# Weighting the experts' outputs on GpSimd and summing them with one reduction per chunk on VectorE

## The reference

```python
xc = depthwise_conv(x, dw_kernel) + dw_bias                   # 3 taps along the sequence
x1 = x + silu(xc @ pw_w.T + pw_b)
logits = x1 @ router_w.T + router_b                           # 8 experts
top_v, top_i = top_k(logits, 2); top_w = softmax(top_v)
rw = sum(one_hot(top_i, 8) * top_w[..., None], axis=-2)       # 8 weights per token, 6 of them zero
ye = silu(einsum('bsd,eod->bseo', x1, expert_w) + expert_b)   # all 8 experts, dense
combined = einsum('bse,bseo->bso', rw, ye)                    # <- the part that is changed
h = rmsnorm(x1 + combined @ out_w.T + out_b) * norm_w
y = h + gelu(h @ ff_down_w.T + ff_down_b) @ ff_up_w.T + ff_up_b
x = layernorm(x + y)
```

## Time and profile before

| | us |
|---|---|
| three runs, median (lowest to highest) | 3467.42 (3454.39 to 3469.43) |
| profiled execution | 3465.11 |
| its span, first to last instruction | 3463.2 |
| last instruction of `combine`, chunk 0, ends | 2450.20 |
| last instruction of `combine`, chunk 15, ends | 2715.57 |

### The profile page before, as it was taken

One profiled execution on the slowest core, in us unless ns is written; L12 is line 12 of the kernel. 1 busy time (PEld: TensorE's weight loads), 2 busy tenths in 40 slices (PEclk: granted clock), 3 DMA queues, 4 the chain that ended last, 5 costly groups with the idle time before them and its releaser, 6 DMA issues. The chain is left out here.

```text
span 3463.2 us, 83326 instructions
## 1 busy us (share of the span) xinstructions
PE 2800.7 (81%) x28622; PEld 1991.1 (57%) x28638; DVE 2189.8 (63%) x5986; ACT 1821.4 (53%) x3448; POOL 1835.0 (53%) x1742
## 2 busy tenths in 40 slices
PE   2999858988888799826459997996988669996993
PEld 2999746745555466514336664664445436664893
DVE  3122466568887588751458886777899767886124
ACT  0555446445555566502136665775566767662551
POOL 5742764357776555444655545664033755554626
PEclk9999989989998899955579998998899989997997
DMA  9888612001100221117411112221000011222884
GB/s 334 264 261 243 194 50 12 3 27 41 39 36 37 70 78 64 61 51 187 128 41 51 61 46 95 81 88 58 1 1 1 3 29 57 77 67 82 249 255 121
DMA packets 325161, 315.42 MB, mean 91 GB/s; under 512 B 111350, under 2 KB 244889, under 8 KB 324508
## 3 DMA queue, kind: packets, MB, share of 16 engines
q1 hardware_dynamic: 283244, 261.98, 24.6%
q0 software_dynamic: 16384, 33.59, 3.3%
q10 hardware_dynamic: 25264, 16.40, 1.6%
HBM read 167.28 MB, written 60.69 MB: 66 GB/s over the span
## 5 line engine op out<-in xcount | busy, mean ns | idle before, releaser
L938 DVE TENSOR_TENSOR moe_first_tile_y<-moe_first_out_ps,moe_first_expert_w 128x256 f32<-128x256 f32 x85 | 36.0, 424 | 245.5 <-PE moe_first_out_ps L1074 245.5
L1871 POOL TENSOR_TENSOR causal_k_blocks<-causal_k_T,headmask 128x1024 f32<-128x1024 f32 x64 | 121.4, 1899 | 99.6 <-PE causal_scores L1481 94.0
L1871 POOL TENSOR_TENSOR alibi_k_blocks<-alibi_k_T,headmask 128x1024 f32<-128x1024 f32 x64 | 121.3, 1897 | 94.8 <-PE alibi_scores L1481 91.0
L796 POOL DMA_INDIRECT moe_first_token_y<-slot_y,moe_first_slots x128 | 125.2, 978 | 82.4 <-DMA slot_y<-moe_first_tile_y 44.1
L1074 PEld LDWEIGHTS moe_first_out_ps<-moe_first_expert_w,moe_first_hid 128*128 128x128 f32 x1360 | 164.9, 192 | 4.3
L1871 POOL TENSOR_TENSOR full_k_blocks<-full_k_T,headmask 128x1024 f32<-128x1024 f32 x64 | 120.8, 1898 | 85.0 <-PE full_scores L1481 80.0
L1074 PE MATMUL moe_first_out_ps<-moe_first_expert_w,moe_first_hid 128*128 128x128 f32 x1360 | 165.2, 275 | 0.0
L1147 POOL DMA_INDIRECT slot_x<-x_tok,moe_first_slots x128 | 123.9, 968 | 67.3 <-issue 38.1
L3164 PE MATMUL L_ffn_experts<-weights_odd,x_T 128*128 128x512 f32 x256 | 143.1, 643 | 12.4 <-ACT L_ffn_expert_out L3264 11.3
L1871 POOL TENSOR_TENSOR keys_k_blocks<-keys_k_T,headmask 128x1024 f32<-128x1024 f32 x64 | 120.9, 1900 | 46.0 <-PE keys_scores L1481 42.4
L3087 DVE SCALAR_TENSOR_TENSOR L_ffn_combined<-L_ffn_expert_out,L_ffn_mix,L_ffn_combined 128x128 f32<-128x128 f32 x448 | 138.9, 372 | 4.0
(11 more groups left out here) (580 smaller groups left out, 9079.8 us busy)
## 6 DMA issues: line engine op xcount, KB each, us to landing
moe_first_expert_w<-in_L_attn_experts SPq DMA_DIRECT2D x85, 578.0 KB
moe_last_expert_w<-in_L_ffn_experts SPq DMA_DIRECT2D x53, 578.0 KB
moe_first_tile_x<-slot_x SPq DMA_DIRECT2D x85, 128.0 KB, 4.7
slot_y<-moe_first_tile_y SPq DMA_DIRECT2D x85, 128.0 KB
slot_x<-blank ACTq DMA_DIRECT2D x2, 4992.0 KB, 40.4
L_ffn_tile_x<-slot_x SPq DMA_DIRECT2D x32, 256.0 KB, 3.4
slot_y<-L_ffn_tile_y SPq DMA_DIRECT2D x32, 256.0 KB
moe_last_tile_x<-slot_x SPq DMA_DIRECT2D x53, 128.0 KB, 4.0
```

What stands on the lines that cost most here:

```text
L796: pool.indirect_dma_start(y_in[:, p, k, r, :], None, slot_y[part][0:NTS[part] * SLOT_TILE, :], bass.IndirectOffsetOnAxis(slots[:, part, r, ...
L938: dve.tensor_tensor(y_out[:, q, :, :], out_bank[j % 2][:, 0:SLOT_TILE].rearrange("p (s d) -> p s d", s=SPAN), over(wall[:, j % RING, 2 * F ...
L1871: pool.tensor_tensor(k_blocks[:, t.p, :, :], keys.to_broadcast([128, 8, TILE]), lanes.to_broadcast([128, 8, TILE]), ALU.mult).then_inc(spr ...
```

## The change

The multiplication leaves VectorE: GpSimd multiplies `expert_out` in place, one 128x1024 operation per tile (`weigh`), four per chunk. VectorE's `combine` becomes one tensor_reduce over the experts, 128x512 from 128x4096, that reads with the expert axis innermost. `mean_square` moves ahead of `combine` in VectorE's list, and `rms` ahead of the first `weigh` in GpSimd's. `comb_done` counts one per chunk instead of eight.

```diff
@@ vector
+                if c >= 2:
+                    dve.wait_ge(weighed, PER * (c - 1))
                 dve.tensor_scalar(mix[:, c % 2, :, :], twice[:, :, :], 0.5, None, ALU.mult).then_inc(mix_done, 1)
             def combine(c):
                 p = c % 2
-                dve.wait_ge(mix_done, c + 1)
-                dve.wait_ge(expert_done, 2 * PER * (c + 1))
                 if c >= 2:
                     dve.wait_ge(combT_ready, c - 1)
-                for e in range(E):
-                    if e:
-                        dve.wait_ge(comb_done, E * c + e)
-                    for k in range(PER):
-                        w = mix[:, p, k, e:e + 1]
-                        if e == 0:
-                            last = dve.tensor_scalar(combined[:, p, k, :], expert_out[:, p, k, e, :], w, None, ALU.mult)
-                        else:
-                            last = dve.scalar_tensor_tensor(combined[:, p, k, :], expert_out[:, p, k, e, :], w,
-                                                            combined[:, p, k, :], ALU.mult, ALU.add)
-                    last.then_inc(comb_done, 1)
+                dve.wait_ge(weighed, PER * (c + 1))
+                dve.tensor_reduce(combined[:, p, :, :], expert_out[:, p, :, :, :].rearrange("p k e d -> p k d e"),
+                                  AX_X, ALU.add).then_inc(comb_done, 1)
-            return [(-4, lambda c: convolve(c) if c else None), (-1, mix_two), (-3, add_pointwise), (0, combine),
-                    (-2, rank), (2, mean_square), (5, residual)]
+            return [(-4, lambda c: convolve(c) if c else None), (-1, mix_two), (-3, add_pointwise), (2, mean_square),
+                    (0, combine), (-2, rank), (5, residual)]
@@ tensor and scalar
-                pe.wait_ge(comb_done, E * c + E)
+                pe.wait_ge(comb_done, c + 1)
-                        act.wait_ge(comb_done, E * (c - 1))
+                        act.wait_ge(comb_done, c - 1)
@@ gpsimd
-            return [(4, rows_with_residual), (2, rms), (5, inverse_std)]
+            def weigh(c, k):
+                p = c % 2
+                pool.wait_ge(mix_done, c + 1)
+                pool.wait_ge(expert_done, 2 * (PER * c + k + 1))
+                pool.tensor_tensor(expert_out[:, p, k, :, :], expert_out[:, p, k, :, :],
+                                   spread_last(mix[:, p, k, :], D), ALU.mult).then_inc(weighed, 1)
+
+            return [(2, rms), (0, lambda c: weigh(c, 0)), (0, lambda c: weigh(c, 1)), (4, rows_with_residual),
+                    (0, lambda c: weigh(c, 2)), (0, lambda c: weigh(c, 3)), (5, inverse_std)]
```

More of the change, by code:

```diff
@@ L3001, in conv_moe @@
         expert_ready, expert_done = sem("experts_ready"), sem("experts_done")
-        comb_done = sem("combined")
+        weighed, comb_done = sem("experts_weighed"), sem("combined")
         combT_ready, combT_copied, z_ready, squared = sem("combT_ready"), sem("combT_copied"), sem("z_ready"), sem("squared")
```

## The result

| | before | after |
|---|---|---|
| median of 4 runs (lowest to highest), us | 3467.53 (3454.39 to 3469.43) | 3664.84 (3660.76 to 3667.60) |
| profiled execution, its span | 3465.11, 3463.2 | 3660.76, 3658.4 |
| granted TensorE clock, mean over the span | 0.895 | 0.871 |
| end of `combine`, chunk 0 and chunk 15 | 2450.20, 2715.57 | 2443.60, 2910.03 |

The changed kernel takes 1.0577 times as long (95% interval 1.0549 to 1.0605), 197 us more; forecast were 3679 us and a range of 3610 to 3725.

What follows compares the result with a forecast made beforehand. VectorE, 97% busy in a steady round of 19.7 us, was taken to set the pace. Terms of 14.0, 2.2, 7.6, 3.7 and 0.1 + 7.1 give 34.7 us a round; 3465.1 + 212 = 3677, median 3679, range 3610 to 3725.

Steps and rivals of the forecast that it cites:

- The cover that the change takes away: On VectorE, combine(i)'s 10 us and the work ahead of it hid the 11.05 us from combine(i-1) to square(i-2).
- the loop: combine, turn_combined, output, square, mean_square, rms, weighs, next combine: closes over one round without overlap, 34.7 us against 19.7.
- the things that cost nothing: inverse_std on GpSimd and GpSimd's conflicts with VectorE, both said to add no time.
- The clock term: End of combine to end of square: 11.05 us at full clock, taken as 14.0 with TensorE returning at half clock.
- The strided reduction: VectorE's tensor_reduce stepping 128 floats: 7.1 us, between bounds of 4.4 without penalty and 8.5 with twice each element's time.
- GpSimd's price: One weigh, a 128x1024 multiplication on GpSimd: 1.90 us, so 7.6 us a chunk.
- the sum: Round lengths added up: 26 for round 2, 31 for round 3, eleven of 34.7, 27.7 for round 15; 212 us more.
- The signs that the prediction named: combine ends some 34 us apart; GpSimd waits some 15 us before ms_eps; VectorE, TensorE wait over 10; reduction 7.1.
- the contiguous rate: Rival: VectorE's reduction takes 4.4 us instead of 7.1, giving 3636 us; chance 0.20.
- larger terms: Rival: half clock for the whole stretch from combine to square, and 8.5 us for the reduction: 3719 us; chance 0.15.
- the other side: Rival: no loop closes, the busiest engine sets the pace, 16 to 19 us a round, about 3435 us; chance 0.05.
- Exclusive use of the memory by one of the two engines: Rival: no loop, but GpSimd shuts out VectorE's two-input operations: 19 us a round, 3460 to 3470 us; chance 0.03.

Runs made afterwards that it cites:

- e9: Changed kernel with rms put behind the weighs on GpSimd, mean_square left ahead of combine: 3525.16 us, ratio 1.0196 to the kernel before.
- e4: Kernel before, its multiplications still on VectorE, with only mean_square moved ahead of combine: 3520.84 us, ratio 1.0165 to the kernel before.
- e1: Changed kernel with mean_square put back behind rank on VectorE and rms behind the weighs on GpSimd: 3539.54 us, ratio 1.0222 to the kernel before.
- e8: Changed kernel with 70 unread products added on TensorE before turn_combined, in rounds 3 to 14 only: 3638.29 us, ratio 1.0523 to the kernel before.
- e2: Changed kernel with rows_with_residual moved behind the fourth weigh on GpSimd: 3624.43 us, ratio 1.0465 to the kernel before.
- e6: e1 with GpSimd's list as four weighs, rms at lag 3, inverse_std at lag 6, then rows_with_residual: 3445.86 us, ratio 0.9964 to the kernel before.
- e7: e6 with the eight experts' values side by side in memory, ScalarE writing with a step of 8 floats: 3442.60 us, ratio 0.9951.
- e3: Changed kernel with the reduction summing 8 neighbouring floats, so its output is not right: 3619.16 us, ratio 1.0453 to the kernel before.
- e5: Changed kernel with 60 unread products added on TensorE before turn_combined in every round: 3664.67 us, ratio 1.0597 to the kernel before.

## Why the prediction was right

The mechanism was the one forecast, and so were its terms; the steady round from the timelines of before and after:

| term | forecast | measured |
|---|---|---|
| end of combine to end of square | 14.0 | 13.91 (2580.63 to 2594.54) |
| mean_square and rms | 2.2 | 2.12 (to 2596.66) |
| four weighs | 7.6 | 7.5 |
| rows_with_residual | 3.7 | 3.6 |
| handoff and reduction | 7.2 | 7.1 |
| round | 34.7 | 34.20 |

- The cover that the change takes away was read from two places: 11.05 us from `combine` to the square, and the order of GpSimd's list. e9 shows that the second of them closes the loop; e4 shows that the first alone costs 56 us where `combine` is still long. The prediction had named both moves together and not told them apart, nor named the second loop through `inverse_std`, which it put among the things that cost nothing. Beside the longer loop it does cost nothing; with that one open (e1, e9) it sets the round.
- The clock term was taken at its upper value, from one round of before. It holds in all steady rounds (0.70 granted), and e8 measures its share as 2.7 us a round.
- The strided reduction was sized by the nearest row, a two-input operation with one operand at a step of 32 floats: 7.1 forecast, 7.03 measured, and 4.42 for the contiguous one (4.4 forecast). The Trainium skill's rule of 16-byte lines (Advanced Engine Details and Errata, SBUF Cachelines) speaks for this side. The trace agrees: steps of 32 and of 128 floats, both beyond a line, cost 0.66 and 0.64 ns per element. That a two-input product and a reduction would pay the same was taken over without a row for it, and came out; the runs show the size and not why. The upper bound of 8.5 for twice the time of each element should have been 8.7 by the prediction's own figures, which changes nothing here.
- GpSimd's price was that of the same form elsewhere: 1.897 forecast, 1.900 measured.

The forecast lay 14 us too high by the medians, 16 by the profiled executions, and all of that is in the sum. Round 3 was put at 31 and took 28.0, since its square came 11.4 us after `combine` and not 14. The windows from `combine` to the square, in round 3 and in a steady round of the kernel after:

```profile
2484.10:2495.46 11.36, 11.10 (x44) 6.84 (x46) 5.04 (x27) 5.75 (x13) 0.00 (x0) 0.85 0.01 1
2580.63:2594.54 13.91, 13.64 (x44) 8.15 (x46) 6.96 (x35) 8.99 (x16) 2.36 (x4) 0.67 0.00 1
```

As many products, at 0.85 instead of 0.67: this part of the miss is the clock's. In e2 round 3 took its 13.96 us to the square, at 0.67. Rounds 13 and 14 were counted as full ones (69.4) and took 63.1, as the chunks ahead run out: 43 and 35 products to the square instead of 44, in 12.07 and 10.47 us, the same two times as in e2. The nine rounds from 4 to 12 took 0.5 each less than the sum, 4 to 5 us. Rounds 1, 2 and 15 hit within 1.3 each. And chunk 0 ended at 2443.60, not 2448.5, since the first `convolve` of the stage began 5.6 us earlier than in the profiled execution of before (2402.01 against 2407.57), which the change does not touch; of the 2 us that chunk 0 was to gain, 1 is left.

The signs that the prediction named all came, one with another size: GpSimd was to wait some 15 us before ms_eps. It waits 8.5 there in the steady round, and 10.7 more for `residual` ahead of `inverse_std`.

The rivals: the contiguous rate is excluded by the reduction's 7.03; larger terms by 13.91 and 7.03 (half clock does not double the first term). The loop was there; without it (e6) a round takes 17.5, so the case of the other side was rightly built, and needed only a list that allows it. Exclusive use of the memory by one of the two engines was put at no change. Without the loop (e6) it is there again, 1.8 us on L3069 and L3073 in the round shown and some 10 us in all 15, but the round is 17.5 and not 19.

## What to carry to other kernels

Before work is moved to an idle engine, write down in which order each in-order engine meets its stages, and follow from the end of the moved step to what waits for it, and on to what waits for that: if the path comes back to the step's start within a round, its terms add up, however idle each engine is. Such a loop shows in the waits as a circle of releasers. The busy shares alone don't tell: in the kernel after no engine is above 57% of a round, in the short loop of e4 VectorE is at 18.14 of 20.78. It is opened by order and lag, which cost nothing here but some 7.5 us at the end of the stage; what the moved work is worth (here 0.4%) is only seen then. Of several loops only the longest counts, so opening one shows the next.

## What the runs showed of the hardware

- ScalarE's activation of 128x512 from PSUM to SBUF takes 601 ns written contiguously and 1134 ns written with a step of 8 floats. GpSimd's in-place product of 128x1024 took 1922 ns with the weight the same for 128 neighbours, and 2389 ns where each neighbour has another weight of the eight (e6, e7). The shortest of each were 1889 and 2335 ns, so the difference is not one of waiting beside VectorE.
- The reduction has one input and still took 7.36 us beside GpSimd's products (e6) against 7.03 alone. The Trainium skill (SBUF — State Buffer, Who interferes with whom) says that a VectorE instruction with at most one SBUF input, outside the modes that use two ports, does not contend with GpSimd. The 7.36 against 7.03 is 5% off that, and not a single case: the median of 16 is 7350 against 7032 ns. The reduction that reads side by side shows nothing of it, 4412 ns in e7 and 4420 alone in e3; but in e7 it runs beside `rows_with_residual` and in e6 beside the weighs. Whether the strided reading or the weighs make the difference was not tried. For two-input operations the rows bear the page out, 1.20 against 0.19 us for L3069.
- TensorE came back at the lower level after waits of 3.65 and 3.67 us and at the upper one after 3.24 in e5, and in the kernel before at either level after nearly equal waits of 2.87 and 2.89 us. In e4 it came back at the lower level after six waits of 3.93 us and at the upper after a seventh of 3.93. Nor did the level of the first row tell how long it lasts: in e5 the transposes at 2559.59 took 1.12 us behind a wait of 4.51, and the round took 31.5. Behind equal waits of 13.07 us the stretch from `combine` to the square in round 3 ran at a mean of 0.85 in the kernel after and of 0.67 in e2. What decides it was not settled; e4, e5 and e8 only give its price.
